# Splitting a two-bank scan in two, with its decays handed over bank by bank, in a hand-ordered two-layer kernel

## The reference

```python
dA = jnp.exp(jnp.einsum('bld,dn->bldn', delta, A))          # 256 channels, 16 states
dBu = jnp.einsum('bld,bln,bld->bldn', delta, Bm, u)
...
def step(carry, inp):
    a, bu, c = inp
    carry = a * carry + bu
    y = jnp.einsum('bkdn,bkn->bkd', carry, c)
    return (carry, y)
```

## Time and profile before

| what | value |
|---|---|
| median of 3 runs | 1466.05 us (1443.38 to 1468.54) |
| profiled execution | 1452.7 us, its span 1451.0 us |
| PE busy | 1144.1 us, 79% of the span |
| DVE busy | 1000.1 us, 69% |
| ACT busy | 680.0 us, 47% |
| POOL busy | 601.7 us, 41% |
| mean granted clock of PE | 0.816 of 2.4 GHz |

### The profile page before, as it was taken

One profiled execution on the slowest core, in us unless ns is written; L12 is line 12 of the kernel. 1 busy time (PEld: TensorE's weight loads), 2 busy tenths in 40 slices (PEclk: granted clock), 3 DMA queues, 4 the chain that ended last, 5 costly groups with the idle time before them and its releaser, 6 DMA issues.

```text
span 1451.0 us, 12541 instructions
## 1 busy us (share of the span) xinstructions
PE 1144.1 (79%) x4326; PEld 666.5 (46%) x4326; DVE 1000.1 (69%) x1607; ACT 680.0 (47%) x1034; POOL 601.7 (41%) x314
## 2 busy tenths in 40 slices
PE   0647889879989897888798798889678776866866
PEld 0425655645547354554445363545335342432425
DVE  2232435377766788877977857899779899698722
ACT  1132445464645545847382555655643624633330
POOL 0012121264543547544553535554655746365210
PEclk9957578777977888979997798979869789797865
DMA  3000000133340335323323323343345445356100
GB/s 92 1 7 8 1 0 8 54 130 116 123 140 29 124 106 162 119 94 116 116 97 123 116 66 118 117 145 117 125 145 174 147 155 175 115 173 210 58 7 8
DMA packets 50840, 142.80 MB, mean 98 GB/s; under 512 B 6741, under 2 KB 17241, under 8 KB 50777
## 3 DMA queue, kind: packets, MB, share of 16 engines
q1 hardware_dynamic: 50776, 142.01, 29.8%
...
## 4 chain that ended last, share of the span: by engine, by line
PE 39%; DVE 34%; ACT 12%; issue 7%; POOL 5%; DMA 2%; SPq 1%; POOLq 0%; DVEq 0%; ACTq 0%
DVE hs L858 14%; PE mp L1200 7%; PE yp L1299 6%; DVE hs L861 5%; PE mp L1191 5%; PE fp L1116 3%; PE fp L1130 3%; ACT he L974 3%; PE fp L1124 2%; POOL dbu L563 2%; ACT L883 2%; DMA bcast<-held 2%; ACT dA L1068 2%; DVE eo L780 2%; DVE f_z L651 2%
## 5 line engine op out<-in xcount | busy, mean ns | idle before, releaser
L563 POOL TENSOR_TENSOR dbu<-du,bcast 128x1024 f32<-128x1024 f32 x128 | 372.3, 2912 | 334.3 <-DVE hs L858 224.3
L1299 PE MATMUL yp<-hs,ident 128*128 128x512 f32 x512 | 300.0, 718 | 75.6 <-DVE hs L861 75.4
L858 DVE TENSOR_TENSOR_SCAN hs<-dA,dbu 128x1024 f32<-128x1024 f32 x128 | 292.5, 2285 | 51.4 <-PE yp L1299 34.7
L1068 ACT ACTIVATE dA<-delta,mA 128x496 f32<-128x496 f32 x256 | 162.9, 669 | 202.7 <-DVE hs L858 201.9
L1299 PEld LDWEIGHTS yp<-hs,ident 128*128 128x128 f32 x512 | 105.7, 223 | 219.5 <-DVE hs L861 112.3
L861 DVE TENSOR_TENSOR hs<-hs,bcast 128x1024 f32<-128x1024 f32 x128 | 175.6, 1372 | 4.4
L1200 PE MATMUL mp<-w_e,he 128*128 128x64 f32 x1024 | 153.8, 323 | 13.7 <-ACT he L974 11.9
L1200 PEld LDWEIGHTS mp<-w_e,he 128*128 128x128 f32 x1024 | 152.3, 238 | 26.5 <-ACT he L974 17.1
L1191 PE MATMUL mp<-cont,w_e 64*128 64x512 f32 x256 | 123.6, 836 | 34.9 <-DVE lg L737 25.1
L974 ACT ACTIVATE he<-mp,vectors 128x512 f32<-128x512 f32 x128 | 82.3, 682 | 90.4 <-PE mp L1191 89.9
L883 ACT ACT_TABLE_LOAD x75 | 96.2, 1283 | 1.3
...
## 6 DMA issues: line engine op xcount, KB each, us to landing
bcast<-held SPq DMA_DIRECT2D x128, 1024.0 KB, 5.4
...
```

What stands on the lines that cost most here:

```text
L563: pool.tensor_tensor(out=dbu[:, j % 2, :].rearrange("p (r t) -> p r t", r=2), in0=d, in1=b_n, op=ALU.mult).then_inc(dbu_r.sem, 1)
L858: dve.tensor_tensor_scan(out=h, data0=dA[:, :], data1=dbu[:, j % 2, :], initial=0.0, op0=ALU.mult, op1=ALU.add).then_inc(hs_r.sem, 1)
L1068: ins = act.activation(out=dst, in_=src, func=ACT.Exp, scale=mA[:, c, 2 * k + r:2 * k + r + 1])
L1299: last = pe.matmul(yp[:, :], lhsT=ident[:, :], rhs=hs[:, j % 2, r * SEQ:(r + 1) * SEQ], start=(k == 0 and r == 0), stop=(k == PAIRS - 1 an ...
```

## The change

- The scan of a pair becomes two scans of 512 columns, one for each state and bank of `dA`. On DVE the first half, the second half and the multiply are three steps of S in place of one. The multiply waits for both halves.
- On ACT each decay activation is a step of its own, waits for the scan half that used its bank one pair earlier (`hs_r >= j - 1`, with j now counting states), and signals `dA_r` itself.
- `dA_r` and `hs_r` count twice as fast; POOL's wait is rewritten and is still for both halves of step j - 2.
- The strings of `ORDER` are new for all five engines.

```diff
     "DVE":
-        "FFFFFFFFFFFFFFMFMFFFMFMFFMFFMFMMFFFMFMMMPMPFFFFMMFFFFMFMMMPFFFMFMMMMPPPSFSFFSFMMSSFFSSMFMFMFMSPSSSMM"
+        "FFFFFFFFFFFFFFMFMMMFFFFMMMMFFFFMFMMPPFFFMFPMMFFFFMMMMPFSFSFSFMFMSSSMSSPSSPSSSSSSSFSSFFMFMSPSSSSSSSS"
...
-        dA_r = signal("dA_r", STEPS)
+        dA_r = signal("dA_r", 2 * STEPS)
...
-        hs_r = signal("hs_r", STEPS)
+        hs_r = signal("hs_r", 2 * STEPS)
...
                             if j >= 2:
-                                pool.wait_ge(hs_r.sem, j - 1)
+                                pool.wait_ge(hs_r.sem, 2 * (j - 1))
...
+                            for r in range(2):
+                                yield True
+                                dve.wait_ge(dA_r.sem, 2 * j + r + 1)
+                                if r == 0:
+                                    dve.wait_ge(dbu_r.sem, j + 1)
+                                    if j >= 2:
+                                        dve.wait_ge(sum_ps.sem, j - 2 + 1)
+                                half = slice(r * SEQ, (r + 1) * SEQ)
+                                dve.tensor_tensor_scan(out=hs[:, j % 2, half], data0=dA[:, half],
+                                                       data1=dbu[:, j % 2, half], initial=0.0,
+                                                       op0=ALU.mult, op1=ALU.add).then_inc(hs_r.sem, 1)
                             yield True
-                            dve.wait_ge(dA_r.sem, j + 1)
-                            dve.wait_ge(dbu_r.sem, j + 1)
-                            if j >= 2:
-                                dve.wait_ge(sum_ps.sem, j - 1)
+                            dve.wait_ge(hs_r.sem, 2 * (j + 1))
                             h = hs[:, j % 2, :]
-                            dve.tensor_tensor_scan(out=h, data0=dA[:, :], data1=dbu[:, j % 2, :], initial=0.0,
-                                                   op0=ALU.mult, op1=ALU.add).then_inc(hs_r.sem, 1)
-                            dve.wait_ge(hs_r.sem, j + 1)
                             dve.tensor_tensor(out=h, in0=h, in1=bcast[:, j % SLOTS, 1, :],
                                               op=ALU.mult).then_inc(hc_r.sem, 1)
...
-                        for k in range(PAIRS):
-                            s = c * PAIRS + k
-                            j = i * STEPS + s
+                        for n in range(STATES):
+                            j = (i * IC + c) * STATES + n
                             yield True
-                            if s == 0:
+                            if c == 0 and n == 0:
                                 act.wait_ge(delta_r.sem, delta_r.at(i, 1))
                             table(ACT.Exp)
-                            if j >= 1:
-                                act.wait_ge(hs_r.sem, j)
-                            for r in range(2):
...
+                            if j >= 2:
+                                act.wait_ge(hs_r.sem, j - 1)
...
+                            act.activation(out=dst, in_=src, func=ACT.Exp,
+                                           scale=mA[:, c, n:n + 1]).then_inc(dA_r.sem, 1)
```

More of the change, by code:

```diff
@@ L39 @@
     "SP":
[L40 to L41 removed]
+        "AAABBBBABBBBBBBBBBABBBBBBBBBBBBBBBBABBBBBBBBBBBBDABBBBBBBBBBBBBBBBBDABBBBBBBBBBBBBBBBBDBBBBBBBBBBBBB"
+        "BBBBBDBBBBBBBBBBBBBBBBBBBBBBDBBBBBBBBDBBBBBBBBBBBBDD",
     "Pool":
[L43 to L44 removed]
@@ L45 @@
-        "SSPSSMSMSMSSPSSPSSSSSMSMSMSSSSSSSSSMMMMM",
+        "FFFFFFMFFFMMPFFMPFFPSSSFMMSSPSSFSFMSSSFSFPSSSFPSSMSMFFMSPSSSSPSSSSFSFSPSFMSMMSSSFFSPSMSMSFMSFSPSSFSP"
+        "MSMSSMFFSSSSSPSMSMSMFSPFSPSSSFMMMSSSSFSFSSSPSMSMSMSFPSFSPSSFSMSMSFSMSSSSSSPSMMSSMSSSPSSSSSPSSMSMMSSP"
+        "SSSSSPMSMSMSPSSSSSMSMMSSSSSSSSSSMSMSSMMM",
     "DVE":
-        "FFFFFFFFFFFFFFMFMFFFMFMFFMFFMFMMFFFMFMMMPMPFFFFMMFFFFMFMMMPFFFMFMMMMPPPSFSFFSFMMSSFFSSMFMFMFMSPSSSMM"
-        "SFMSFMSMFSSSFMMMMMMSPPPMSMPSMMFSMFFSFSMMFSFSFFSMMMFMSSPSSMMSFMSFMSFSMSFSPPPSMMPSMMMMFFFSFSMSMFFMMFMF"
@@ L59 @@
-    "PE":
[L60 to L65, removed]
+        "FFFFFFFFFFFFFFMFMMMFFFFMMMMFFFFMFMMPPFFFMFMPMMFFFFMMMMPFSFSFSFMFMSSSMSSPSSPSSSSSSSFSSFFMFMSPSSSSSSSS"
@@ new lines @@
+        "SSFSFFSFSSSSSMFMFSSFMFMFMMSSSPSSSSMSMSSFSSMFFMFMSPPSSSPSSSSSSSSSSSSPSSSSMMSSSSSSSSFSFSMMFMFMSSPSFSFS"
+        "FSFMFMSSSSMMSMSSSSSSSFFFMFMSSMSPMMMSSSPSSSMPSMSSSFMMFMSSFSSFSPSSSSMFMFSSFSFMFMMMSSSPSSSMSSMSSSSMMFMS"
+        "FFSFSSSSSMMSSSSSSMMSSMSPMPSSSPSSMSMSSSSMMFMSFSPSSSFMFMSSSPSMMSSMMFSFSSFSFMFMSSSMMSSMSSSSSSSSSSFSFFSF"
+        "MMSSSSSMMMSSMSPPSSSPSMSMSSSSSMMSMSPFSSFSFSMFMSSPSSMSSMSSFMFMFSFSSFSMSSMSSSSSSSMFMFMSSSSSSSSSSMMSSSSS"
+        "MSMMMSSSPSPSSMSSSMSSSPMMSSMSSSSSPSSSSSSSSSSMSMSSSSMSSMSMMSSSPSSSSMSSMSPSSSMMSSMSPSSSPSSSSMMSSSSSMSMM"
@@ new lines @@
+        "MSSPSMSSMSSSSSMMSMSPSSSSSSSSMMSSSSSMMMMSSSMSSMSPSSSMMSSMSSSSSSSSSSMSSSMSSSSMMSSSMSSSMSSSSSSMSSSMSSSM"
+        "SSSSSSSSPMMMMMMMMMMM",
+    "ACT":
+        "FFFFFFFFFFFFFFFFFFMFMFFMFMFFFMMMMFFFMFMMFFFFFFFPPPPPFMFFMFFPFFPMPPMMMMMPPPFFFMSFSSMSMFSSFFSFFSFFSSPS"
+        "PSSSSPPPFMFFSFFSFFSSMPSSSMPSPMFSPFFSSMFMMMSPSPPFFFMFSSMFSFSFSMSSMFSMFFSPSPSMSSPSSPSPPSMPSPPSSMMFFMFF"
+        "SSPMSSPSPSFFFMSSFMSSFMSFFSFFSFFSMSMSMSSMMMMMFSSFFMFSSMFSFSPFPMSSPPMSSMPPMSPSPMFPFFSSMFMMSMSPPPFFFMFS"
+        "SMFFSSFSMSSSMMSMFSMFSSFMMMSSMFSSFFFSSMMSSPSPSMPSSPPPMSMPSPMPSMSMPMPMPMSSFFFSSMFMSSMFSSFFSMFMFSSFSFMS"
+        "SSSMSMMFMSFMSSFFSFMSMSFPSPFSMSPSSPPPSMSMPPMSPSMPPMPMSMSMFSFFSSFMSMSFSFFFFSFFSSMSSSMMSSMSSMSSMMMMSSSS"
+        "MMSSSSSSMSSPPSPMSMSSPPMSPSMPSPSPSSMMSMMSPSSPPSSMSSMSSSMSSSSMSMMSSPMSSMMMPMSSPSSPPSMSPMPPPPSMSPPSSSMS"
+        "MMSSSMSMMSMMSSSMSMSSMSSSSMSMMSSSMSMSSMSSMMSSSSSSMMSSSSSSMSSSSMMMMMMMMMMM",
@@ new lines @@
+    "PE":
+        "FFFFFFFFFFFFFFFFFFFFFFFMFMFMFMFFFFMFMMMMMFMFMFMMFMFFFFFFFPFFPPFPFMFFMPFFPMFFMMFMMMPMPMMMFFMFMFMSFFSF"
+        "FFSFFFSPFSPSPFPFMFFSSFFFFFMSSPMFPFSMFMSPMMMFMPMMMFFMFSMFSMFFFSFFSPFMFMSPSPSPSPMPSPSMMSMFMFPFMFFSFFPS"
+        "MMSMMFFMFSMFMSFFSFFFFFFMSMSMFSMMMMMFMPMMMFMFSMFMSFFFPFSFPSPPMMSPMFPFSMMSMFMFMPMPSMMFMFMFMFMSFFFSFFSM"
+        "SMFMFSMSMFFMMMSMMSMPMFFFMFMSMPSPFPSPSMPMPMSMMPMPMMFSMMFSMMFMMSFMFSFSFFMSMFFFFSFMSSMMMFMFMSFMMMSMPFMF"
+        "MSMPSPFFFSPSPFMPMPSMPMPMSMFMMMFSMSMMFFMMSMFFFFSFFFFSFSMSMSMSMMSMMMPMSMMMMMSMSSSPPSMPSSMPMPSPSMMSMPMM"
+        "MSPMSMMMSMSMSPSSMMSMSMMMSMPMPMPMMMSSMPMPMSPPPSSMMSMSMMMSMMSMMMMSMMMSPSSMMSMSMMSMSMMSMMSMMSMMSMSSSSSS"
@@ L1055, in s_thread @@
                     for c in range(IC):
-                        for k in range(PAIRS):
-                            s = c * PAIRS + k
-                            j = i * STEPS + s
+                        for n in range(STATES):
+                            j = (i * IC + c) * STATES + n
                             yield True
-                            if s == 0:
+                            if c == 0 and n == 0:
                                 act.wait_ge(delta_r.sem, delta_r.at(i, 1))
                             table(ACT.Exp)
-                            if j >= 1:
-                                act.wait_ge(hs_r.sem, j)
-                            for r in range(2):
[L1066 to L1073, removed]
+                            if j >= 2:
+                                act.wait_ge(hs_r.sem, j - 1)
+                            dst = dA[:, n % 2 * SEQ:(n % 2 + 1) * SEQ].rearrange("p (k t) -> p k t", t=CHUNK)[:, :, 1:]
+                            src = delta[:, i % 2, c, :].rearrange("p (k t) -> p k t", t=CHUNK)[:, :, 1:]
+                            act.activation(out=dst, in_=src, func=ACT.Exp,
+                                           scale=mA[:, c, n:n + 1]).then_inc(dA_r.sem, 1)
             side_by_side(ORDER["ACT"], F=f_thread(), M=m_thread(), P=p_thread(), S=s_thread())
```

9 lines of the change are left out of this document (removed).

## The result

The changed kernel takes 1373.5 us (median of 4 runs, 1364.35 to 1376.46); the kernel before took 1462.0 us in the same comparison. The ratio is 0.946, with a 95% interval of 0.935 to 0.957: 5.4% faster. A second session gave 0.943 (0.935 to 0.952). Executions more than 1.5% above the quickest of the same kernel are left out of the ratios, so a ratio can differ a little from that of the medians beside it. The forecast was 2.5% less than before and 1430 us, with a range down to 1385 us. The direction was right, and the forecast size was less than half of the measured one.

What follows compares the result with a forecast made beforehand. No engine was full: in the scan stretch DVE and PE, each about four fifths busy, wait for each other. Terms 12 + 24 - 12.6 - 27 - 14 - 5 = -22.6 took 1452.7 to 1430 us; range 1385 to 1480.

Steps and rivals of the forecast that it cites:

- The split: Scans on DVE: two halves cost more than one whole scan, 17.7 us of DVE's time, 12 us on the path.
- Multiplies behind `dbu`: DVE multiplies issued after POOL's `dbu` wait at the SBUF port: 33 of 65 at 1.1 us, some 24 us on the path.
- Late decays: DVE's idle waits before scans for ACT's decays, nine waits, taken as gone by the bank-wise handing over: -12.6 us.
- Waits of PE: PE waits less for ACT (-15 us) and for DVE's short steps (-12 us) through finer steps: -27 us, the softest term.
- The five rows: PE's three largest waits for ACT and its waits for DVE's `lg` and `f_z`, 61 us in all, bounding the gain.
- Head: Before the first scan: steps leave DVE's and PE's head, the scan comes 34 us earlier, DVE idles 14 us less.
- tail: After the last scan: three M steps now stand ahead of it, -5 us, leaving a tail of 75 us.
- three signs of being wrong: Multiply's mean staying at 1.37 us, multiply's mean passing 1.9 us, or DVE's fill in the stretch not about 86%.
- the second rival: Multiplies lose the SBUF port race to `dbu`: 58 us on the path, +38 in sum, 1491 us; chance 0.12.
- the first (DVE stays at 81%): Scan stretch: finer steps give nothing, only the amount of DVE's work counts, fill stays 0.81, 1466 us; chance 0.26.
- The third: Scan stretch: queues mesh much better, DVE and PE both reach 90%, 1356 us, or 1390 us at 87%; chance 0.16.

Runs made afterwards that it cites:

- e8: The changed kernel with the multiply moved up directly behind the scan only in the 14 pairs where it took over 1.4 us: 1378.7 us, ratio 0.954.
- e1: The changed code with the order of before, so the split without the new order: 1455.0 us, ratio 1.008 to the kernel before.
- e3: The changed kernel with every multiply moved up to stand directly behind the second scan half: 1394.1 us, ratio 0.965 to the kernel before.
- e9: The letters of e5, but with whole scans and each decay waiting for the whole scan before: 1412.4 us, ratio 0.973 to the kernel before.
- e2: The code of before (whole scans, both decays in one step) with the new order: 1423.1 us, ratio 0.986 to the kernel before.
- e5: The changed kernel with the second scan half moved up directly behind the first in 38 pairs: 1386.8 us, ratio 0.960 to the kernel before.
- e7: The changed kernel with 65 random swaps of neighbouring letters in DVE's string, none with a multiply: 1425.5 us, ratio 0.985 to the kernel before.
- e12: A second draw of e7's 65 random swaps in the changed kernel's DVE string: 1422.4 us, ratio 0.979 to the kernel before.
- e10: The changed kernel unaltered, run again as the mark of a later session: 1370.5 us, ratio 0.943 to the kernel before.

## Why the prediction was too small

The sum was -22.6 us against the profiled execution; its counterpart of after is 80 us faster. The forecast had the first scan at 270 us and a tail of 75 us, which leaves 1083 us for the stretch. Measured are 274, 70 and 1027 us: the whole miss of 57 us lies in the stretch.

By the forecast's account (span = DVE busy + DVE idle) it is sharper still. The forecast put DVE's busy time up by 54 us, to some 1050 us, and so its idle time at 375 us; measured are 997.7 busy and 373.6 idle. **The step that failed is the cost side: DVE's busy time, up 18 us for the split and 36 us for the multiplies, with 36 us of the two on the path. It fell by 2 us.** Such an account adds up whatever the cause, so it says where the miss stands and not that each us of DVE is a us of time: e8 has 9 us less of DVE's busy time than the kernel after and is no faster.

- **The split, forecast +17.7 us busy, +12 on the path.** The row was right (1.214 for 1.210 us). In busy time it is 10.4 us, since neighbouring halves overlap, and in direct succession a pair is 0.12 us shorter than before. e1's loss is near my term; in the new order nothing of it can be seen.
- **Multiplies behind `dbu`, forecast +36 us busy, +24 on the path.** The mechanism is there (e3), but of the 65 multiplies not 33 but 14 took over 1.4 us, and the multiplies cost 18.6 us more. The forecast said that "the multiply alone pays", and so put the other DVE steps at nothing. They pay too. In the kernel before, `dbu` often started with the multiply, and the step behind the multiply ended only with it. Here both end at 1128.7 us:

```profile
1125.34 3.32 POOL L563 TENSOR_TENSOR dbu<-du,bcast 128x1024 f32<-128x1024 f32 x1 [1.24 <-DVE hs L858]
1126.37 2.31 DVE L645 SCALAR_TENSOR_TENSOR d_nb<-d_mv,d_rs 128x4 f32<-128x4 f32 x1
```

The median `d_nb` takes 0.16 us, so this one held some 2.1 us of waiting. The groups of two such steps, before and then after:

```profile
L651 DVE TENSOR_SCALAR f_z<-fx,f_mv,f_rs 128x128 f32<-128x128 f32 x64 | 33.5, 583 | 3.6 <-POOL f_rs L482 3.4
L645 DVE SCALAR_TENSOR_TENSOR d_nb<-d_mv,d_rs 128x4 f32<-128x4 f32 x16 | 15.5, 967 | 17.0 <-POOL d_rs L482 16.8
```

```profile
L655 DVE TENSOR_SCALAR f_z<-fx,f_mv,f_rs 128x128 f32<-128x128 f32 x64 | 26.5, 474 | 4.7 <-POOL f_rs L486 4.5
L649 DVE SCALAR_TENSOR_TENSOR d_nb<-d_mv,d_rs 128x4 f32<-128x4 f32 x16 | 7.5, 471 | 4.8 <-POOL d_rs L486 4.2
```

All DVE steps but scan and multiply take 22.6 us less together (some rose: `m_vv` by 6.4 us). With 9 us more of overlap between neighbours, that makes good the 10.4 and the 18.6 us. By these rows the wait was for the most part handed from one step to another.

- **Late decays, forecast -12.6.** Wrong in sign: the wait rose to 18.6 us. It is 64.8 us when the split is taken out of the same order (e9), so the hand-over doesn't remove the old order's waits; it lets the new order run closer to the decays.
- **Waits of PE, forecast -27.** The five rows held 61.4 us and hold 55.1 now. The two for DVE's short steps fell by 12 us, as forecast, but by the order and not by the finer steps: `lg`, 25.1 before, is 26.2 in e1 and 2.9 in e2. The three for ACT rose by 6 us instead of falling by 15. What fell instead are two waits that the forecast put at nothing. PE's wait for the multiply, which it didn't list, fell by 40 us, and DVE's wait for `yp`, "on which the change does nothing", by 21. Both fall with the new order alone (e2) and not with the split alone (e1).
- **Head, forecast -14, and tail, -5.** Right in their own terms: DVE's idle time fell by 13 us in the head and by 6 in the tail. The first scan came 30 us earlier, for 34.

That the idle time came out as forecast in total, with most of its rows wrong, is luck. None of the three signs of being wrong came either (the multiply's mean is 1.517 us, the fill 86%), though the forecast was: the fill is a quotient, and DVE's busy time in the stretch (884 us) and the stretch itself were both forecast some 60 us too long. One slip in the sums: in the second rival, 0.7 of 87 us is 61 and not 58.

Of the rivals, the first (DVE stays at 81%) and the second (the race at the port) are refuted for the change as a whole; the fill of 81% is that of e2 and e9 (82% and 81%), where the scan is whole. The third had the right sign: the fill reached 86 to 87%, and its worked point of 87% was 1390 us. It got 0.16 and should have had more: my rivals held the shorter step and the order apart. In the old order the split took 8 us off DVE's idle time before the scans (51.4 to 43.5, e1), in the new one 41 us (75.0 in e9, 33.5 in the kernel after), of which up to 15 us go with moved letters (e5).

What stays open: how much a whole-scan kernel would gain with an order that is written for whole scans with the same care. e2 and e9 take the new order as it is, with letters taken out or made idle, and e7 and e12 show what a disturbed string costs. So the 1.3% of e9 against e5 is shown, and the share of the finer places on top (e5 against the kernel after, 1.5%) is no more than the loss from moving 38 letters, part of which any move may cost.

Open too is PE's clock. The four executions of the kernel after and the four of e10 had a mean granted clock of 0.826 to 0.841 of full speed. The kernel before, in its 34 executions beside the experiments, had 0.801 to 0.835, and it took 1471 us at the lowest clock and 1426 us at the highest: about 1 us less for each 0.001. So the clock goes with the time from one execution to the next, and differences of 1% between kernels (e8) are within what it does. It is not the gain: between 0.826 and 0.836, eight executions of the kernel before took 1426 to 1445 us, and seven of the changed one 1364 to 1376. The means are 65 us apart. Whether the remaining 15 us come by the clock, and whether it rises because the queues mesh or the other way round, no run shows.
